# Expert tiles of two sizes in a routed SwiGLU stage: 39 tiles of 256 slots become 25 of 256 and 21 of 128

## What is computed

```python
def _L0_ffn_ref(x, Wg, W1, W2, W3):          # x: (32, 128, 256), hidden width 512
    logits = jnp.einsum('bsd,de->bse', x, Wg)
    top_vals, top_idx = jax.lax.top_k(logits, 2)
    probs = jax.nn.softmax(top_vals, axis=-1)
    ...
    for e in range(8):
        u = jnp.einsum('bsd,dh->bsh', x, W1[e])
        v = jnp.einsum('bsd,dh->bsh', x, W2[e])
        h = u * jax.nn.sigmoid(u) * v
        y = jnp.einsum('bsh,hd->bsd', h, W3[e])
        out = out + y * weights[..., e][..., None]
    return out
```

## Time and profile before

| | |
|---|---|
| time, median of 3 runs | 1529.22 us (1528.43 to 1530.22) |
| the profiled execution's own time | 1524.42 us |
| its span in the trace | 1522.0 us |
| PE busy over the span | 1220.0 us (80%) |
| DVE, ACT, POOL busy | 1013.8, 728.4, 416.6 us |
| token dispatch (last part, VectorE's row of steps) | from about 500 to 539 us |
| expert tiles, first gather issued to last scatter issued | 540.2 to 876.4 us |

### The profile page before, as it was taken

The page is one execution under the profiler, slowest core; times in us unless marked ns, Lnnn a source line. Parts: engine busy times, 40 slices in busy tenths (PEclk is TensorE's granted clock), DMA queues, the critical chain, the costliest instruction groups (busy, mean ns, idle before and its releaser), DMA issues. The chain is left out here.

```text
span 1522.0 us, 29958 instructions
## 1 busy us (share of the span) xinstructions
PE 1220.0 (80%) x10737; PEld 883.0 (58%) x10737; DVE 1013.8 (67%) x2051; ACT 728.4 (48%) x1402; POOL 416.6 (27%) x403
## 2 busy tenths in 40 slices
PE   4989589898744369999999915883799976999997
PEld 2666456776633359999999803732455542565664
DVE  5999667776654845666666566676788786567553
ACT  4778445554325224444444314034255556756743
POOL 2222255644222035455454311052011111000000
PEclk9999799999985579999999955556899997999999
DMA  7666276666309023232322172001544312133131
GB/s 276 242 238 239 95 146 113 127 108 92 57 30 402 14 70 95 91 95 91 105 95 75 49 268 96 2 1 51 148 80 92 69 25 76 51 127 119 36 126 28
DMA packets 100120, 165.08 MB, mean 108 GB/s; under 512 B 14918, under 2 KB 63882, under 8 KB 98700
## 3 DMA queue, kind: packets, MB, share of 16 engines
q1 hardware_dynamic: 90956, 138.27, 32.5%
q0 software_dynamic: 8640, 24.65, 5.1%
q10 hardware_dynamic: 384, 0.26, 0.1%
HBM read 110.67 MB, written 52.30 MB: 107 GB/s over the span
## 5 line engine op out<-in xcount | busy, mean ns | idle before, releaser
L1545 DVE TENSOR_TENSOR r_sim<-r_pS,r_causal 128x512 f32<-128x512 f32 x128 | 86.2, 681 | 56.0 <-PE r_pS L1455 55.9
L1087 POOL DMA_INDIRECT expert_results<-mt_yout,m_deliver x78 | 77.4, 992 | 150.1 <-ACT mt_yout L1175 138.1
L1120 PE MATMUL mt_pU<-mt_xh,m_w 128*128 128x256 f16 x624 | 116.2, 274 | 1.5 <-DVE mt_xl L1205 1.5
L2971 ACT ACTIVATE q_ex<-q_pE 128x512 f32<-128x512 f32 x128 | 75.7, 600 | 83.3 <-PE q_pE L2590 83.2
L1120 PE MATMUL mt_pV<-mt_xh,m_w 128*128 128x256 f16 x624 | 115.1, 273 | 0.0
L2686 DVE TENSOR_REDUCE q_mx<-q_pS 128x4 f32<-128x512 f32 x128 | 87.1, 685 | 32.1 <-PE q_pS L2569 31.7
L1131 PE MATMUL mt_pY<-m_w,mt_hh 128*128 x624 | 106.4, 273 | 1.0 <-DVE mt_hl L1219 1.0
L3253 PE MATMUL s_pY<-s_w,s_hh 128*128 128x256 f16 x576 | 99.9, 273 | 8.0 <-DVE s_hl L3473 6.6
L1169 ACT ACTIVATE mt_hh<-ahead 128x512 f16<-128x512 f32 x78 | 49.2, 630 | 118.3 <-DVE ahead L1214 118.3
L1079 POOL DMA_INDIRECT mt_xin<-token_rows,m_fetch x78 | 86.2, 1105 | 68.2 <-POOLq L778 44.7
L1211 DVE TENSOR_TENSOR ahead<-mt_pU,ahead 128x512 f32<-128x512 f32 x78 | 53.9, 691 | 58.2 <-ACT ahead L1163 58.2
(11 more groups left out here) (593 smaller groups left out, 3443.6 us busy)
## 6 DMA issues: line engine op xcount, KB each, us to landing
s_spread_share<-shares SPq DMA_DIRECT2D x32, 512.0 KB, 6.0
a_pf<-in_L_ffn_W SPq DMA_DIRECT2D x24, 512.0 KB, 6.6
m_w<-split_w SPq DMA_DIRECT2D x6, 2048.0 KB, 23.2
split_w<-a_ph SPq DMA_DIRECT2D x24, 256.0 KB, 3.8
split_w<-a_pl SPq DMA_DIRECT2D x24, 256.0 KB, 4.2
r_kstack<-k_bounce SPq DMA_DIRECT2D x48, 128.0 KB, 4.0
r_qstack<-q_bounce SPq DMA_DIRECT2D x48, 128.0 KB, 5.3
q_Q<-m_bounce SPq DMA_DIRECT2D x24, 256.0 KB, 7.7
```

The costliest lines, as they stand in the source:

```text
L1087: pool.indirect_dma_start(results[:, :], bass.IndirectOffsetOnAxis(ap=deliver[:, at:at + 1], axis=0), yout[n % 2][:, a, :], None).then_inc ...
L1120: last = pe.matmul(ps[half][:, j, :], W[x][:, e, dc, cols], (xh, xl)[y][p][:, dc, :], start=(m == 0), stop=(m == len(steps) - 1))
L1545: dve.tensor_tensor(sim[n % SIMS][:, :].rearrange("p (h t) -> p h t", t=S), pS[n % 2][:, :].rearrange("p (h t) -> p h t", t=S), repeat(tab ...
L2971: act.activation(ex[n % RING][:, :], pE[n % 2][:, :], ACT.Exp, scale=ATT).then_inc(s["exp"], 1)
```

## The change

`TILES` becomes 46: first `FULL` = 25 tiles of 256 slots, worked as before, then `SMALL` = 21 tiles of 128 slots. These are 71 blocks instead of 78. An expert's rows fill as many whole tiles of 256 as they can (until the 25 are used up), the rest goes into tiles of 128. `dispatch` works out two first slots for each expert (`edges`, `small_base`) and moves the rows that lie past the whole tiles by `jump`.

A small tile takes one indirect DMA in and one out. Its rows are the stationary operand and W1, W2 move with 512 columns: `up_small` has 12 matmuls of 512 columns. u, v and h then stand with rows on the partitions, so the gated rows are turned by four f32 transposes (`turn_hidden`, from `h` into `pU`), their high part and rest are taken from `pU`, and `down_small` has 12 matmuls of 256 columns, into `pY` and `pY2` by turns. The ring of four input buffers and the order scatter(n), gather(n + 4) on POOL are kept.

```diff
+FULL = -(-(2 * B * S - E * (TILE - 1)) // TILE)
+REST = 2 * B * S - FULL * TILE
+SMALL = (REST + E * (P - 1)) // P
+TILES = FULL + SMALL
-BLOCKS = TILES * TILE // P
+BLOCKS = FULL * TILE // P + SMALL
...
-            step(dve.tensor_tensor(more[:, :, :], spread(total[:, :], STEPS), repeat(tile_start[:, 0:STEPS], E), ALU.is_gt))
-            step(dve.tensor_reduce(need[:, :], more[:, :, :], AX, ALU.add))
-            step(dve.tensor_tensor(ahead_of[:, :, :], lower[:, :].rearrange("p (e f) -> p e f", e=E),
-                                   repeat(need[:, :], E), ALU.mult))
-            step(dve.tensor_reduce(need_before[:, :], ahead_of[:, :, :], AX, ALU.add))
-            step(dve.tensor_scalar(base[:, :], need_before[:, :], float(TILE), None, ALU.mult))
-            step(dve.tensor_tensor(at[:, :, :], counts[:, 0:B, :], repeat(base[:, :], B), ALU.add))
+            step(dve.tensor_tensor(more[:, :, :], spread(total[:, :], STEPS), repeat(tile_start[:, 1:STEPS + 1], E), ALU.is_ge))
+            step(dve.tensor_reduce(full[:, :], more[:, :, :], AX, ALU.add))
+            step(dve.tensor_tensor(ahead_of[:, :, :], triangle, repeat(full[:, :], E), ALU.mult))
+            step(dve.tensor_reduce(edges[:, 0, :], ahead_of[:, :, :], AX, ALU.add))
+            step(dve.tensor_tensor(edges[:, 1, :], edges[:, 0, :], full[:, :], ALU.add))
+            step(dve.tensor_scalar(edges[:, :, :], edges[:, :, :], float(FULL), float(TILE), ALU.min, ALU.mult))
+            step(dve.tensor_tensor(in_full[:, :], edges[:, 1, :], edges[:, 0, :], ALU.subtract))
+            step(dve.scalar_tensor_tensor(left[:, :], total[:, :], float(FULL * TILE), in_full[:, :], ALU.add, ALU.subtract))
...
+            step(dve.tensor_tensor(jump[:, :], small_base[:, :], edges[:, 1, :], ALU.subtract))
+            step(dve.tensor_tensor(past[:, :, :], counts[:, 0:B, :], repeat(in_full[:, :], B), ALU.is_ge))
+            step(dve.tensor_tensor(past[:, :, :], past[:, :, :], repeat(jump[:, :], B), ALU.mult))
+            step(dve.tensor_tensor(at[:, :, :], counts[:, 0:B, :], repeat(edges[:, 0, :], B), ALU.add))
+            step(dve.tensor_tensor(at[:, :, :], at[:, :, :], past[:, :, :], ALU.add))
...
             def gather(n):
                 if n >= INPUTS:
                     pool.wait_ge(turned, n - INPUTS + 1)
-                for a in range(BLK):
-                    at = n * BLK + a
+                for a, at in enumerate(blocks(n)):
...
+            def up_small(n, e):
+                k = n - FULL
+                q = 2 * FULL + k
+                pe.wait_ge(xl_done, n + 1)
+                pe.wait_ge(h_done, q - 1)
+                if k >= 2:
+                    pe.wait_ge(hl_done, q - 1)
+                for ps, W, sem in ((pU, W1, u_done), (pV, W2, v_done)):
+                    steps = [(dc, x, y) for dc in range(DC) for y, x in TERMS]
+                    for m, (dc, x, y) in enumerate(steps):
+                        last = pe.matmul(whole(ps[k % 2]), (xh, xl)[y][n % 2][:, dc, 0:P], W[x][:, e, dc, :], start=(m == 0),
+                                         stop=(m == len(steps) - 1))
+                    last.then_inc(sem, 1)
...
+            def turn_hidden(n):
+                pe.wait_ge(h_done, 2 * FULL + k + 1)
...
+            def down_small(n, e):
+                pe.wait_ge(hl_done, 2 * FULL + k + 1)
+                pe.wait_ge(y_copied, max(n - 1, FULL))
...
+            for n in range(FULL, TILES):
+                e = pe.value_load(owner[0:1, n:n + 1], min_val=0, max_val=E - 1)
+                up_small(n, e)
+                if n == FULL:
+                    down(FULL - 1, 1, before, False)
+                else:
+                    turn_hidden(n - 1)
+                if n + 1 < TILES:
+                    transpose(n + 1)
+                if n >= FULL + 2:
+                    down_small(n - 2, second)
+                second, before = before, e
+            turn_hidden(TILES - 1)
+            down_small(TILES - 2, second)
+            down_small(TILES - 1, before)
...
+            for n in range(FULL, TILES):
+                sigmoid_small(n)
...
+                    hidden_high_small(n - 1)
+                if n + 1 < TILES:
+                    high(n + 1, (n + 1) % 2, True)
+                if n >= FULL + 2:
+                    result_small(n - 2)
...
+                    gate_small(n)
+                    if n > FULL:
+                        hidden_low_small(n - 1)
+                    if n + 1 < TILES:
+                        low(n + 1, (n + 1) % 2)
```

More of the change, by code:

```diff
@@ new lines, in _ @@
+            parts = REST // P
+            step(dve.tensor_tensor(more[:, :, 0:parts], spread(left[:, :], parts),
+                                   repeat(tile_start[:, FULL:FULL + parts], E), ALU.is_gt))
+            step(dve.tensor_reduce(small[:, :], more[:, :, 0:parts], AX, ALU.add))
+            step(dve.tensor_tensor(ahead_of[:, :, :], triangle, repeat(small[:, :], E), ALU.mult))
+            step(dve.tensor_reduce(small_base[:, :], ahead_of[:, :, :], AX, ALU.add))
+            step(dve.tensor_scalar(small_base[:, :], small_base[:, :], float(P), float(FULL * TILE), ALU.mult, ALU.add))
@@ L1006, in _ @@
                                   ALU.mult).then_inc(s["held_turn"], 1)
-            step(dve.tensor_tensor(passed[:, :, :], spread(tile_start[:, :], E - 1), repeat(base[:, 1:E], TILES),
-                                   ALU.is_ge))
+            for tiles, bounds in ((slice(0, FULL), edges[:, 0, 1:E]), (slice(FULL, TILES), small_base[:, 1:E])):
+                step(dve.tensor_tensor(passed[:, tiles, :], spread(tile_start[:, tiles], E - 1),
+                                       repeat(bounds, tiles.stop - tiles.start), ALU.is_ge))
             step(dve.tensor_reduce(owner_f[:, :], passed[:, :, :], AX, ALU.add))
@@ L1050, in expert_tiles, with blocks, landed, items @@
     piece_high, piece_low = c.sem("piece_high"), c.sem("piece_low")
+    def blocks(n):
+        return [2 * n, 2 * n + 1] if n < FULL else [FULL * BLK + n - FULL]
+    def landed(n, ring):
+        return 16 * sum(len(blocks(m)) for m in range(n % ring, n + 1, ring))
+    def items(n):
+        return 2 * (n + 1) if n < FULL else 2 * FULL + n - FULL + 1
+    def whole(t):
+        return t[:, :, :].rearrange("p a t -> p (a t)")
     def piece_due(n):
@@ L1135, in down @@
                 last.then_inc(down_done, 1)
+            def up_small(n, e):
[12 more added lines that the diff above has]
+            def turn_hidden(n):
+                k = n - FULL
+                pe.wait_ge(h_done, 2 * FULL + k + 1)
+                for j in range(HC):
+                    at = slice(j * P, (j + 1) * P)
+                    last = pe.transpose(whole(pU[k % 2])[:, at], whole(h[k % 2])[:, at], ident[:, :])
+                last.then_inc(h_turned, 1)
+            def down_small(n, e):
+                k = n - FULL
+                pe.wait_ge(hl_done, 2 * FULL + k + 1)
+                pe.wait_ge(y_copied, max(n - 1, FULL))
+                for j in range(HC):
+                    for m, (x, y) in enumerate(TERMS):
+                        last = pe.matmul((pY, pY2)[k % 2][:, 0, :], whole((hh, hl)[x][k % 2])[:, j * P:(j + 1) * P], W3[y][:, e, j, :],
+                                         start=j == 0 and m == 0, stop=False, skip_group_check=True)
+                last.then_inc(down_done, 1)
             transpose(0)
             before = None
-            for n in range(TILES):
+            for n in range(FULL):
                 e = pe.value_load(owner[0:1, n:n + 1], min_val=0, max_val=E - 1)
@@ L1148, in _ @@
                 before = e
-            down(TILES - 1, 1, before, False)
+            second = None
+            for n in range(FULL, TILES):
[6 more added lines that the diff above has]
+                if n + 1 < TILES:
+                    transpose(n + 1)
+                if n >= FULL + 2:
[4 more added lines that the diff above has]
+            down_small(TILES - 1, before)
         @block.scalar
@@ L1188, in step @@
                     result(n - 1, k - 1 + p, 1 - p, not starts(n, 1) and not starts(n, 2))
-                if not starts(n, TILES - 1):
-                    high(n + 1, 1 - p, age > 0)
+                high(n + 1, 1 - p, age > 0)
                 sigmoid(n, 1, age == 0)
```

88 lines of the change are left out of this document (66 added, 22 removed).

## The result

The changed kernel takes 1551.8 us (median of 4 runs, 1547.34 to 1552.28) where the kernel before takes 1528.89 (1528.43 to 1530.22): a ratio of 1.0142, 95% interval 1.0122 to 1.0162. It is slower, by 22.9 us. The forecast was 17 us more, 1546. The profiled executions say the same: 1547.34 us with a span of 1545.4, against 1524.42 and 1522.0. One run of experiment 8 took 1623.46 us at a mean granted clock of 0.77, where its five others had 0.88; its median and ratio are of the five.

What follows compares the result with a forecast made beforehand. TensorE's row of matmuls bounds the stage before; a ring of gather, result and scatter bounds the small tiles. Stage +14.6 us and dispatch +2.3 make +17, taking the median from 1529.2 to 1546; range 1531 to 1565.

Steps and rivals of the forecast that it cites:

- TensorE's own work: Matmuls and transposes of a small tile, 4.56 us; 20 us less in all if TensorE is never kept waiting.
- The ring: Small tiles: transpose, last result matmul, result copy, scatter issue, gather, next transpose; 6.55 us a round, bounds 6.4 to 7.1.
- flight: Time of a gather from issue to landing, taken as 2.8 us in every round of the ring.
- The idle time in it: TensorE idle in each small tile between turning the hidden rows and the next transpose, 2.0 us, 17 times.
- The gate chain: Second and third small tiles: up, turned hidden rows, high part, rest, next rows' rest, handoffs; 5.1 us each.
- Sixteen rounds of 6.55: From tile 29's transpose at 20.3 us after tile 25's first matmul to tile 45's at 125.1.
- the clock rival: TensorE's granted clock falls in small tiles: 1561 us if in a third of the rounds, 1589 if in all; 15%.
- Dispatch: VectorE steps before the stage: 12 more steps, partly offset by smaller ones, net +2.3 us.
- The case of the other sign: Rival: gathers are not late and the gate chain sets 5.1 us for every small tile; 1522 us; 8%.
- The 1512 given for a dense TensorE: Rival: TensorE stays dense in the small tiles and the 20 us are nearly all won; 1512 us; 3%.
- The longer ring of 7.3 us: Rival: the ring takes longer than its rows, 7.3 us, 13 us more over 17 rounds; 1559 us; 7%.

Runs made afterwards that it cites:

- experiment 8: The kernel of 7 with the next tile's expert number loaded on TensorE right behind `up`, a tile earlier: 1511.33 us, ratio to before 0.9911.
- 7: Changed kernel, small tiles' gathers up to six tiles ahead and before the scatter, unused slots spread, engine order remade for the gate chain: 1508.54 us, ratio to before 0.9896.
- 9: The kernel of 7 with the gather of tile 28 issued ahead of the last large tile's scatter: 1505.02 us, ratio to before 0.9862.
- 1: Changed kernel with gather(n + 4) issued ahead of scatter(n) on POOL in small tiles: 1515.26 us, ratio to before 0.9923.
- 2: Changed kernel with six input buffers in place of four, order on POOL unchanged: 1516.92 us, ratio to before 0.9953.
- 3: Changed kernel with one more indirect DMA, of rows nobody reads, ahead of each small tile's gather: 1580.2 us, ratio to before 1.0353.
- 6: Kernel before, all tiles of 256 slots, with gather(n + 4) ahead of scatter(n) on POOL: 1527.79 us, ratio to before 1.0016.
- experiment 4: Changed kernel with six spare matmuls of 512 columns ahead of each transpose from the fourth small tile on: 1548.75 us, ratio to before 1.0148.
- experiment 5: Changed kernel with unused slots fetching different rows instead of all row 0, two more VectorE steps: 1544.61 us, ratio to before 1.0115.

## Why the prediction was right, step by step

- **TensorE's own work, 4.56 us a small tile; 20 us to be won.** Shown by 7, at 4.555. With nothing in the way the stage takes 315.3 us from first gather to last scatter (9: 543.05 to 858.37), 20.9 less than before.
- **The ring, 6.55 us.** Measured 6.565, and the terms hold one by one in the round at 797.92: transpose to the end of the last result matmul 1.75 (forecast 1.69), hand-off 0.04, copy 0.38, to POOL 0.27, scatter issue 1.51 here and 1.29 in others (787.30 to 788.59; forecast 1.30), flight and hand-off 2.75 (forecast 2.85). The flights in the twelve rounds are 2.7 to 3.0 us, about the 2.8 of the row; whether VectorE held a gather back was not tested. Experiments 1, 2 and 3 took the ring apart at two places and lengthened it at a third, and each time the time followed.
- **The idle time in it, 2.0 us, 17 times.** The count is right, the mean is 1.55 us. Between the last result matmul of one tile (799.40 plus 0.109) and the next `up` (799.81) lie 0.3 us that the forecast took as nothing. They hide in the ring and cost no time. Another 0.17 us is a matter of counting: the trace shows the four turnings of the hidden rows as 0.60 us long, of which the forecast counts 0.43, from start to start.
- **The gate chain, 5.1 us.** 5.03 in 1 and 2. Tile 26's `up` started 5.57 us behind tile 25's (forecast 5.65), tile 27's another 5.03 (forecast 5.1); tile 29's transpose 20.64 us after the first matmul of tile 25, forecast 20.3.
- **Sixteen rounds of 6.55: the term that was too small.** Tile 29 to 45 took 109.7 us (778.29 to 888.01), not 104.8. Twelve rounds were right, the last four took 30.9 us instead of 26.2: the flight of 3.6 us in place of 2.8 is 3.2 of it, and most of the rest is the clock rival in small, from 864.5 to 868.5 us. The prediction took one flight for all gathers, though the last tiles fetch other data than the rest. This is 5 of the 6 us that the forecast missed. From tile 45's transpose to the last scatter it was 10.6 us, forecast 10.1.
- **Dispatch, +2.3.** From the counts to the first gather 30.2 us became 32.6 (509.96 to 540.18, 509.46 to 542.03). As forecast.
- **The rest.** From the last scatter's issue to the next stage it was 8.22 us and is 6.64 (6.6 to 7.2 in the other kernels with small tiles, but 8.3 in 3; 8.1 in 6): 1.6 us won that the forecast had not seen. The last scatter of before is the second of a pair and now stands alone; that can't be all of it, since it stands alone in 3 too, and the cause stays open. The stages behind take 640.1 us where they took 637.4. They are the same code, and take 636.6 (8) to 640.3 us (1) in the other kernels, so this is not put down to the change.
- **The rivals.** The case of the other sign was put at 1522; when the ring was opened, the time was 1515 on a chip where before takes 1527. The 1512 given for a dense TensorE compares with 1508.5 and 1505. The clock rival was right in kind: the clock fell twice, behind gaps of 2.29 and 2.24 us, and lengthened one round to 8.61 us and the other only to 7.57. The longer ring of 7.3 us did not happen in the twelve rounds, but the last four came to its length by another way, the repeated row.

## What to carry to other kernels

When a loop's work per step shrinks, go once round every ring of buffers and queues in it with the new durations: a wait that cost nothing at 8.3 us a tile (a gather queued behind a scatter that needs a late result) set the pace at 4.6 us of work. The repair was two lines or two buffers, and worth 29 to 33 us. A change that seems to lose may only be issued in the wrong order: the rows gave 4.56 us of work and 6.55 us of waiting, and that difference was the profit to look for.

## What the runs showed of the hardware

- An indirect gather of 128 rows of 1 KB took 2.7 to 3.0 us from issue to landing in the ten gathers from 790 to 855 us, and 3.6 us, each of eight times in two kernels, when all 128 indices named the same row; different indices for the unused slots brought it back to 2.6 to 2.8. Different rows alone do not keep it there: the gathers issued 0.9 us behind two DMAs of 256 KB from SyncE's queue took 4.1 us (at 782.69 us in experiment 4) and 3.5 (at 782.16 in experiment 5), and the same gather at the same place 2.8 in the changed kernel. What decides there was not tested.
- The granted clock stayed at 1.00, the 2.4 GHz level, through twelve rounds of 6.6 us, each with one idle gap of 1.3 to 1.6 us and one of 0.3. In the ring of the changed kernel and of experiments 3 and 5 it fell to 0.50, the 1.2 GHz level, for part of a round, always in or behind a gap of 2.17 us or more (2.29 and 2.24 in the changed kernel, 2.17 in 5, 2.6 to 4.1 in 3). Other gaps of 2.0 to 3.0 us left it at 1.00 (2.16 in the changed kernel, 2.56 and 2.97 in 3), so the length of the gap alone does not tell; what decides was not settled. A low clock in such a ring makes the result later, and with it the next gather.
- One indirect DMA costs POOL 1.27 to 1.30 us from issue to issue, and added in the ring it cost that and no more as long as the clock held.
